# Probabilities as weights, values streamed: the value products of a sliding-window attention turned round

## What is computed

```python
# 16 query heads, 2 key/value heads, head size 16, window of 64 keys around each query
q = (x @ Wq + bq).reshape(b, s, NUM_HEADS, HEAD_DIM).transpose(0, 2, 1, 3)
k = (x @ Wk + bk).reshape(b, s, NUM_KV_HEADS, HEAD_DIM).transpose(0, 2, 1, 3)
v = (x @ Wv + bv).reshape(b, s, NUM_KV_HEADS, HEAD_DIM).transpose(0, 2, 1, 3)
...
scores = jnp.einsum('bgrsd,bgswd->bgrsw', qg, k_win)
probs = jax.nn.softmax(scores, axis=-1)
out = jnp.einsum('bgrsw,bgswd->bgrsd', probs, v_win)
out = out.reshape(b, NUM_HEADS, s, HEAD_DIM).transpose(0, 2, 1, 3).reshape(b, s, DIM)
return out @ Wo + bo
```

## Time and profile before

| | |
|---|---|
| median of 3 runs | 3582.03 us (3581.8 to 3582.57) |
| the profiled execution | 3582.19 us, span 3580.5 us |
| granted TensorE clock, mean | 0.996 |
| TensorE busy | 3415.3 us, 95% of the span |
| TensorE weight loads busy | 2296.7 us, 64% |
| VectorE busy | 2586.4 us, 72% |
| ScalarE busy | 1890.3 us, 53% |
| GpSimd busy | 1255.6 us, 35% |

### The profile page before, as it was taken

One profiled execution on the slowest core, in us unless ns is written; L12 is line 12 of the kernel. 1 busy time (PEld: TensorE's weight loads), 2 busy tenths in 40 slices (PEclk: granted clock), 3 DMA queues, 4 the chain that ended last, 5 costly groups with the idle time before them and its releaser, 6 DMA issues. The chain is left out here.

```text
span 3580.5 us, 89270 instructions
## 1 busy us (share of the span) xinstructions
PE 3415.3 (95%) x34684; PEld 2296.7 (64%) x34684; DVE 2586.4 (72%) x6184; ACT 1890.3 (53%) x4167; POOL 1255.6 (35%) x1457
## 2 busy tenths in 40 slices
PE   3999999999999999999989999999999999999998
PEld 2666666666666666666656666666666666666666
DVE  4677777777677776777767777777777767777677
ACT  1465463645636455464644646546365563646546
POOL 3524334232342424325233252433424234242432
PEclk9999999999999999999999999999999999999999
DMA  3101010010100101001010010101001010010100
GB/s 89 25 14 48 2 41 21 14 48 2 48 13 18 44 14 36 14 24 38 14 37 13 24 38 14 48 2 47 15 15 47 2 48 13 18 44 14 37 14 25
DMA packets 91023, 97.16 MB, mean 27 GB/s; under 512 B 19825, under 2 KB 73697, under 8 KB 90593
## 3 DMA queue, kind: packets, MB, share of 16 engines
q1 hardware_dynamic: 90592, 91.35, 9.6%
HBM read 74.01 MB, written 17.30 MB: 26 GB/s over the span
## 5 line engine op out<-in xcount | busy, mean ns | idle before, releaser
L834 POOL TENSOR_TENSOR qx<-qx 128x512 f32<-128x512 f32 x256 | 278.2, 1091 | 684.6 <-ACT qx L1081 683.7
L1344 DVE TENSOR_REDUCE row_max<-bank 128x4 f32<-128x384 f32 x512 | 271.9, 549 | 146.3 <-PE bank L1742 146.3
L1211 DVE TENSOR_TENSOR am<-bank,causal 128x512 f32<-128x512 f32 x512 | 328.2, 683 | 42.1 <-PE bank L1585 42.1
L1436 DVE TENSOR_TENSOR sq_lo<-qx,sq_hi 128x512 fp32r<-128x512 f32 x256 | 208.1, 813 | 193.1 <-ACT sq_hi L1060 192.6
L949 ACT ACTIVATE tanh_g<-bank 128x256 f32<-128x256 f32 x128 | 49.0, 383 | 405.7 <-PE bank L1474 405.7
L1474 PE MATMUL bank<-w_vg,xt 128*128 128x512 f32 x512 | 252.3, 615 | 0.0
L828 POOL TENSOR_TENSOR xl<-xt,xh 128x1024 fp32r<-128x1024 f32 x32 | 75.3, 2354 | 464.9 <-DVE xh L1406 464.9
L1515 PE MATMUL bank<-xt,w_down 128*128 128x512 f32 x512 | 237.2, 596 | 0.0
L1862 PE MATMUL bank<-sq_hi,pj_t 128*128 128x512 f32 x512 | 214.9, 420 | 16.4 <-DVE sq_lo L1436 9.9
L1353 DVE TENSOR_TENSOR am<-bank,row_max 128x384 f32<-128x384 f32 x384 | 212.8, 554 | 9.8
L999 ACT ACTIVATE am<-am 128x384 f32<-128x384 f32 x384 | 201.9, 526 | 9.9 <-DVE am L1353 3.3
(11 more groups left out here) (263 smaller groups left out, 8827.0 us busy)
## 6 DMA issues: line engine op xcount, KB each, us to landing
g_wide<-gate_rows SPq DMA_DIRECT2D x64, 512.0 KB, 6.4
qt<-in_L_attn_x SPq DMA_DIRECT2D x136, 128.0 KB, 2.3
x<-in_L_attn_x SPq DMA_DIRECT2D x128, 128.0 KB, 2.2
out<-x SPq DMA_DIRECT2D x128, 128.0 KB, 1.7
x<-in_L_ffn_w_fc SPq DMA_DIRECT2D x1, 1024.0 KB, 5.8
attn<-in_L_ffn_w_proj SPq DMA_DIRECT2D x1, 1024.0 KB, 8.0
w_up<-in_L_ffn_Wu SPq DMA_DIRECT2D x1, 512.0 KB, 5.8
w_down<-in_L_ffn_Wd SPq DMA_DIRECT2D x2, 256.0 KB, 3.7
```

Of the source, the lines that this page charges most:

```text
L834: nc.gpsimd.tensor_tensor(sq[:, n % 3, :], relu[:, n % 3, :], relu[:, n % 3, :], ALU.mult)\
L1211: nc.vector.tensor_tensor(am_tiles[:, :, j], bank[3 + j][:].rearrange("p (f e t) -> p f e t", f=2, e=2), causal[:].unsqueeze(1).unsqueeze( ...
L1344: nc.vector.tensor_reduce(row_max[:, j, :], bank[1 + j][:, 0:4 * KW].rearrange("p (h k) -> p h k", k=KW), AX.X, ALU.max, negate=(j == 0)). ...
L1436: nc.vector.tensor_tensor(sq_lo[:, n % 3, :], sq[:, n % 3, :], sq_hi[:, n % 3, :].bitcast(F32), ALU.subtract)\
```

## The change

The roles in `values` are swapped. The turned probabilities are the weights: 96 keys x 32 queries of one head. The values are streamed: 17 columns. There is one product per head and block, 64 for a chunk in place of 16. The four blocks go to the four groups of 32 partitions of bank 7, and the result stands there by query, with heads in the order in which `values_turn` left them. `values_out` and `values_turn` go, with their semaphores oc_ok and xp_ok. VectorE's `attention_out` reads bank 7 itself, 17 columns a head in place of 32. Because bank 7 is then read until the division is done, `window_values` of the later parts goes to bank 0, and TensorE gets new waits: values of chunk c for the division of chunk c-1, the turn of window values for the bias of the chunk before, and `attention_turn` for both that bias and the copy of the window values.

```diff
-    v2 = sb("v2", [P, NW * 2 * V1 + DV - V1])
+    v2 = sb("v2", [P, NW * 2 * V1])
...
@@ ScalarE
-                    def values_out(c):
-
-                        act.wait_ge(s["pv_ok"], at("pv_ok", c + 1))
-                        if c:
-                            act.wait_ge(s["xp_ok"], at("xp_ok", c))
-                        nc.scalar.copy(o2_t[:].rearrange("p r b q -> p b r q"),
-                                       bank[7][:].rearrange("p (b r q) -> p b r q", b=4, q=WB)).then_inc(s["oc_ok"], 1)
-
...
@@ VectorE
-                        turned = bank[7][0:KW, :].rearrange("p (a d) -> p a d", d=2 * DH)
+                        turned = bank[0 if part else 7][0:KW, :].rearrange("p (a d) -> p a d", d=2 * DH)
...
-                        dve.wait_ge(s["xp_ok"], at("xp_ok", c + 1))
+                        dve.wait_ge(s["pv_ok"], at("pv_ok", c + 1))
...
-                        o_bank = bank[0][:].rearrange("p (h d) -> p h d", d=DV)
+                        o_bank = bank[7][:, 0:H * V1].rearrange("p (h d) -> p h d", d=V1)
...
@@ TensorE
-                        if c >= 4:
-                            pe.wait_ge(s["oc_ok"], at("oc_ok", c))
-                        for b in range(4):
-                            for g in range(2):
-                                for i in range(2):
-                                    rows = slice(64 * g + 32 * i, 64 * g + 32 * i + 32)
-                                    first = ((4 * c + b) * 2 + g) * V1
-                                    mm = nc.tensor.matmul(bank[7][rows, b * P:(b + 1) * P], v2[0:KW, first:first + DV],
-                                                          pr_t[c % 2][0:KW, 8 * i + g:8 * i + 8:2, b * WB:(b + 1) * WB],
-                                                          start=True, stop=True)
+                        if c:
+                            pe.wait_ge(s["o2_ok"], at("o2_ok", c))
+                        for i in range(2):
+                            for l in range(2):
+                                for t in range(2):
+                                    for g in range(2):
+                                        place = ((2 * l + t) * 2 + g) * 2 + i
+                                        for b in range(4):
+                                            rows = slice(b * WB, (b + 1) * WB)
+                                            first = ((4 * c + b) * 2 + g) * V1
+                                            mm = nc.tensor.matmul(bank[7][rows, place * V1:(place + 1) * V1],
+                                                                  pr_t[c % 2][0:KW, 8 * i + 4 * l + 2 * t + g, rows],
+                                                                  v2[0:KW, first:first + V1], start=True, stop=True)
                         mm.then_inc(s["pv_ok"], 1)
-
-                    def values_turn(c):
-
-                        pe.wait_ge(s["oc_ok"], at("oc_ok", c + 1))
-                        if c:
-                            pe.wait_ge(s["s2_ok"], at("s2_ok", c))
-                        else:
-                            pe.wait_ge(s["low_ok"], at("low_ok", 2))
-                        for r in range(4):
-                            mm = nc.tensor.transpose(bank[0][:, r * P:(r + 1) * P],
-                                                     o2_t[:, r].rearrange("p b q -> p (b q)"), ident[:])
-                        mm.then_inc(s["xp_ok"], 1)
 
                     def attention_turn(c):
                         pe.wait_ge(s["o2_ok"], at("o2_ok", c + 1))
+                        if c:
+                            pe.wait_ge(s["s2_ok"], at("s2_ok", c))
+                        if c < 3:
+                            pe.wait_ge(s["v2_ok"], at("v2_ok", c + 2))
...
                         values(c)
                         probs_turn(c + 1, 0)
-                        values_turn(c)
                         if c < 3:
+                            if c:
+                                pe.wait_ge(s["s2_ok"], at("s2_ok", c))
+                            else:
+                                pe.wait_ge(s["low_ok"], at("low_ok", 2))
                             window_values(c + 1)
```

More of the change, by code:

```diff
@@ L44 @@
 BIG = -1e30
-DV = 2 * DH
 UNROLL = 8
@@ L184, in build_program @@
     am_flat = am[:].rearrange("p h t -> p (h t)")
-    v2 = sb("v2", [P, NW * 2 * V1 + DV - V1])
-    v2_tiles = v2[:, 0:NW * 2 * V1].rearrange("p (a d) -> p a d", d=V1)
+    v2 = sb("v2", [P, NW * 2 * V1])
+    v2_tiles = v2[:].rearrange("p (a d) -> p a d", d=V1)
     row_max = sb("row_max", [P, 4, 4])
     pr = am_flat[:, 0:H * KW].rearrange("p (j h k) -> p j h k", j=4, k=KW)
-    o2_turned = sb("o2_turned", [P, 4 * P])
-    o2_t = o2_turned[:].rearrange("p (r b q) -> p r b q", r=4, b=4)
     rden = sb("rden", [P, H])
@@ L285, in build_program @@
              "st2 ve2 rs2 xn2_ok xt2p_ok xt2_ok qk2p_ok qk2_ok low_ok v2p_ok v2_ok sc_ok max_ok sub_ok "
-             "pr_ok ptp_ok pt_ok ptd_ok pv_ok oc_ok xp_ok rden_ok o2_ok o2tp_ok o2t_ok s2p_ok s2_ok xh_ok xl_ok tp_ok thi_ok tst_ok h2p_ok "
+             "pr_ok ptp_ok pt_ok ptd_ok pv_ok rden_ok o2_ok o2tp_ok o2t_ok s2p_ok s2_ok xh_ok xl_ok tp_ok thi_ok tst_ok h2p_ok "
              "relu_ok sq_ok sqh_ok sql_ok pj_ok ft_ok ftp_ok tf2_ok f3_ok f4_ok y2_ok gkh_ok gkl_ok nst_ok nve_ok nrs_ok "
@@ L311, in build_program @@
             (8, "qx_ok hm_ok ove_ok ors_ok obet_ok hr_ok din_ok dout_ok dst_ok tg_ok tf_ok ots_ok "
-             "yt_ok qk2_ok oc_ok o2t_ok tf2_ok gsel smid_ok vt_ok sg_ok f1_ok state_ok o1_ok "
-             "onorm_ok y_ok f2_ok x_ok xn2_ok ptd_ok rden_ok o2_ok s2_ok nxn_ok f3_ok f4_ok y2_ok "
-             "hp_ok cum_ok vg_ok f_ok ot_ok otok_ok ytp_ok s_ok pv_ok xp_ok o2tp_ok s2p_ok ftp_ok"),
+             "yt_ok qk2_ok o2t_ok tf2_ok gsel smid_ok vt_ok sg_ok f1_ok state_ok o1_ok onorm_ok "
+             "y_ok f2_ok x_ok xn2_ok ptd_ok rden_ok o2_ok s2_ok nxn_ok f3_ok f4_ok y2_ok hp_ok "
+             "cum_ok vg_ok f_ok ot_ok otok_ok ytp_ok s_ok pv_ok o2tp_ok s2p_ok ftp_ok"),
             (16, "sq_ok relu_ok sqh_ok ost_ok st2 sql_ok nst_ok h2p_ok pj_ok x_in"),
@@ L1049, in _ @@
                             low_rank(1)
-                        values_out(c)
                         exps(4 * c + 6)
@@ L1087, in _ @@
                     relus(1)
-                    values_out(NC - 1)
                     squares(0)
@@ L1712, in window_values @@
                             first = (part * NC + w) * WB
-                            mm = nc.tensor.transpose(bank[7][0:KW, w * QB:(w + 1) * QB],
+                            mm = nc.tensor.transpose(bank[0 if part else 7][0:KW, w * QB:(w + 1) * QB],
                                                      low_t[0:QB, first:first + KW], ident[0:QB, 0:QB])
@@ L1782, in values, with attention_turn @@
                         mm.then_inc(s["pv_ok"], 1)
-                    def values_turn(c):
-                        pe.wait_ge(s["oc_ok"], at("oc_ok", c + 1))
+                    def attention_turn(c):
+                        pe.wait_ge(s["o2_ok"], at("o2_ok", c + 1))
                         if c:
                             pe.wait_ge(s["s2_ok"], at("s2_ok", c))
-                        else:
-                            pe.wait_ge(s["low_ok"], at("low_ok", 2))
-                        for r in range(4):
-                            mm = nc.tensor.transpose(bank[0][:, r * P:(r + 1) * P],
-                                                     o2_t[:, r].rearrange("p b q -> p (b q)"), ident[:])
-                        mm.then_inc(s["xp_ok"], 1)
@@ L1796, in attention_turn @@
-                    def attention_turn(c):
-                        pe.wait_ge(s["o2_ok"], at("o2_ok", c + 1))
+                        if c < 3:
+                            pe.wait_ge(s["v2_ok"], at("v2_ok", c + 2))
                         for k in range(KD):
@@ L1912, in _ @@
                         hidden(n, 1)
-                        if n == 3:
-                            values_turn(NC - 1)
                         if n == 4:
```

## The result

The changed kernel takes 3727.59 us (median of 4 runs, 3718.06 to 3728.75), the kernel before 3581.91. The ratio is 1.0403, 95% interval 1.0385 to 1.0421: slower by 4%, where 3558 us was predicted. The profiled execution took 3718.06 us, 135.9 more than the one of before.

What follows compares the result with a forecast made beforehand. VectorE's loop with the scores was taken to bound chunks 3 to 5, TensorE chunks 0 to 2. Chunk gains of 1.49 us a sequence, times 16, took 23.8 from 3582.0: 3558 us, range 3545 to 3630.

Steps and rivals of the forecast that it cites:

- Bounds of the kernel now: Second attention: a VectorE and score-product loop sets chunks 3 to 5 at 6.21 us; TensorE sets chunks 0 to 2, 6.45.
- the floor of 4.62 + 0.32 + 1.27: Loop period of 6.21 us: VectorE's unbroken work 4.62, then 0.32 until scores start, then 1.27 until the next maxima.
- V = 1.20 us: TensorE's time for a chunk's 64 new value products: 1.08 for 128 records plus 0.12 for tile-shape change, against 1.79 removed.
- 60-column rule: Skill page's claim that a one-column matmul takes as long as about 60 columns; V would be 1.75, the gain gone.
- Chunk 0, 0.59 us: In chunk 0 the loop isn't binding, so TensorE's whole saving of 0.59 us counts.
- New waits at nothing: Waits of values, window-value turn and divided-result turn for division, bias addition and window-value copy: all three cost nothing.
- Last chunk, 0.32 us: Chunk 7, in the feed-forward: values cost 0.19 us more, the removed turn saves 0.51, net 0.32.
- What it adds: Step costing the 64 products a chunk on TensorE, 128 loads and 128 matmul records, by streaming, loading and starting records.
- The slower rival: Start rate of records limits TensorE in the value products: 3665 us at V = 2.54, deciding from V = 1.82; chance 0.16.
- the sum: Gains over a sequence's chunks: together 1.49 us, times 16 sequences 23.8 us.

Runs made afterwards that it cites:

- half-size: The changed kernel with only the first 32 of a chunk's 64 value products, half of the heads left out of the result: 3545.20 us.
- one-pass run: The changed kernel with all 64 value products reading both operands as bf16, one pass each: 3545.29 us once, 3552.27 us timed in rounds (ratio 0.9917).

## Why the prediction was wrong

- **Bounds of the kernel now**: right for chunks 2 to 4. The half-size and the one-pass run show the masks drawn out for VectorE and values 6.21 or 6.22 us apart there, the floor of 4.62 + 0.32 + 1.27. Chunk 5 took 6.34 us as before, and chunk 1 took 6.69 and 6.42.
- **V = 1.20 us**: right, and to the hundredth by luck, since the time of the records was picked between bounds of 0.92 and 2.42. With a packet's edge inside, the values take longer. The records are 186 ns long by the groups, where 180 was estimated. The 60-column rule of the Trainium skill, "TensorEngine Tiling (Array Packing)", section Instruction Overhead, would have made 1.75; the trace shows 1.20.
- **Chunk 0, 0.59 us**: at least that where no edge falls badly. In the fifth sequence of the changed kernel values of chunks 0 and 1 start 5.72 us apart, a gain of 0.73, where 6.45 - 0.59 = 5.86 was forecast:

```profile
1113.34 1.27 PE L1769 MATMUL bank<-v,qx 96*32 96x17 f32 x128
...
1119.06 1.36 PE L1769 MATMUL bank<-v,xn 96*32 96x17 f32 x128
```

- **New waits at nothing**: right. In the changed kernel's list of waits no row names the division, the bias or the copy of window values.
- **Last chunk, 0.32 us**: from the values to the first L1862 it was 257.65 - 254.63 = 3.02 us before; with the changed form there alone 257.13 - 254.44 = 2.69, so 0.33. In all it gave 12.1 us over 16 sequences, 0.75 each: a little later, the first project product behind L1799 starts 0.13 us after it in place of 0.43. I had let the feed-forward merely keep the gain, which was mis-sized.
- **What it adds**: this is the step that failed. V was right; what was missing is a term of its own. It bounded 128 loads and 128 matmuls by streaming, by loading and by starting records, all three read inside groups of at most 64 matmuls. It never asked whether the instructions would be there, and put the time to bring them at nothing. A chunk went from some 300 to some 490; at 3.7 us for 256 that is 4.4 us, under the period of 6.21 to 6.45, and 7.1 us, over it. From one chunk's values to the next it was mostly 6.5 to 7.5 us where no stop over 1 us fell in, and up to 11.8.
- **The slower rival** had the sign and one true reason, "four times as many instructions", but it put the limit into the start of records and let it decide from V = 1.82. V is 1.20, and of the 131.8 us of stops 62.9 came in other groups than the values. It is not what happened.
- **The size**: 132 us of stops, less the 4 of before, less the 24 us of gain that the sum forecast, leave 104 of 136. Two things can make up the rest, and no run parts them. One is the lower clock: the mean clocks allow at most 3716.3 x (1 - 0.983) - 3580.5 x (1 - 0.996) = 49 us, by estimate. The other is stops that hide inside busy groups. Both show in the busy time of the scores, which the change didn't touch: 191.1 us in place of 164.0.

What stays open: what sets the pace of the packets, and why some come later. Between the stops that end at 242.51 and 248.13 us stand 127 matmuls and their loads, one packet, in 5.62 us and not 3.5 to 4. The stops of 2 to 3 us lie there, in chunk 5 of the first sequence with and without the load of x.

## What to carry to other kernels

Cost a change of many small products also by the count: all of TensorE's instructions in a stage, loads and both passes of fp32 included, times 14.5 ns, against the stage's period, and not averaged over the stage, since a slow stretch earned little here for a dense one: some 425 instructions in a period of 6.21 us already lost time. Some packets took longer than 14.5 ns an instruction, so the sum can come out too low. Stops without a named cause in the middle of a uniform group, at equal counts of instructions, were its mark in this trace. Where the layout is wanted, it pays in stages whose other products are long (the last chunk here), or with operands that need a single pass.

## What the runs showed of the hardware

- TensorE's instructions came in packets of 256 (16 KB): 92 more packets for 23552 more instructions, 16 more for 4096. With nothing but small products to run, one came in 3.45 to 4.00 us, 3.46 at a granted clock of 0.50 as at 0.70. 128 instructions put in ahead of the first sequence moved the stop of its chunk 0 by 128 instructions.
- After a stop of 1.30 us inside the masks the granted clock fell from 1.00 to 0.68 and 0.61 in the next 4.6 us; around stops of 0.68 and 0.86 us it stayed at 1.00.
- Loads of 96x32 weights on four column groups with 17 streamed columns ran 128 pairs in 1.20 us, 9.4 ns a pair.
